# Expert layer in two table-driven loops with 64-row slots for the rests, first-layer weights fetched per tile

## The reference, cut to what matters

```python
h = jnp.mod(x_flat[:, :TOP_K].sum(axis=1).astype(jnp.int32), E)      # E = 8, TOP_K = 2
sel = jnp.stack([h, jnp.mod(h + 1, E)], axis=1)
w = jnp.any(sel == e, axis=1).astype(x.dtype) / TOP_K
y = jnp.maximum(x_flat @ W1e + b1e, 0.0) @ W2e + b2e                  # W1e 128x512, W2e 512x128
x = _layernorm(x + _L0_ffn_ref(x, ...))
```

| group | 0 | 1 | 2 | 3 | 4 | 5 | 6 | 7 |
|---|---|---|---|---|---|---|---|---|
| all 2048 tokens | 1052 | 324 | 132 | 35 | 10 | 29 | 131 | 335 |
| first 1536 tokens | 772 | 249 | 101 | 27 | 10 | 26 | 102 | 249 |

## Time and profile before

### The profile page before, as it was taken

The page is one execution under the profiler, slowest core; times in us unless marked ns, Lnnn a source line. Parts: engine busy times, 40 slices in busy tenths (PEclk is TensorE's granted clock), DMA queues, the critical chain, the costliest instruction groups (busy, mean ns, idle before and its releaser), DMA issues.

```text
span 236.5 us, 10737 instructions
## 1 busy us (share of the span) xinstructions
PE 212.2 (90%) x4009; PEld 176.2 (75%) x4009; DVE 147.3 (62%) x521; ACT 120.6 (51%) x360; POOL 117.8 (50%) x219
## 2 busy tenths in 40 slices
PE   6879999999998999998999988999999999999920
PEld 2445778767777667886776678989999999899920
DVE  6836448585877765888898616734655555555540
ACT  3546557765466646765656145754344434344400
POOL 6563034852544427762647601847646545455541
PEclk9999999999999999999999999999999999999995
DMA  4131120112232132130001365212121212121100
GB/s 100 58 94 47 49 96 3 45 52 91 91 78 66 47 103 72 43 96 15 28 25 36 117 201 151 96 38 76 40 62 44 56 43 57 27 48 36 35 22 7
DMA packets 18557, 14.73 MB, mean 62 GB/s; under 512 B 2647, under 2 KB 15547, under 8 KB 18513
## 3 DMA queue, kind: packets, MB, share of 16 engines
q1 hardware_dynamic: 17008, 11.83, 17.9%
q0 software_dynamic: 1216, 2.16, 2.8%
q10 hardware_dynamic: 288, 0.13, 0.3%
HBM read 11.43 MB, written 3.03 MB: 61 GB/s over the span
## 4 chain that ended last, share of the span: by engine, by line
PE 74%; DVE 6%; issue 5%; DMA 4%; POOL 3%; ACT 3%; SPq 1%; POOLq 0%; ACTq 0%; DVEq 0%
PE bS L1308 12%; PE bT L1251 7%; PE bV L1452 6%; PE bV L1459 5%; PE bS L1194 4%; PE bV L1266 4%; PE bS L1219 4%; PE bJ L1170 3%; PE bV L1323 3%; PE bT L1308 3%; PE bS L1233 2%; PE bL L1367 2%; PE bS L1201 2%; PE bV L1274 2%; DMA out<-yo,idx 2%
## 5 line engine op out<-in xcount | busy, mean ns | idle before, releaser
L680 ACT ACTIVATE ha<-bS,b1c 128x128 f32<-128x128 f32 x68 | 19.4, 368 | 38.0 <-PE bS L1308 38.0
L668 ACT COPY PTs<-bT 128x512 f32<-128x512 f32 (+3 forms) x48 | 25.9, 539 | 18.2 <-PE bT L1251 18.2
L567 POOL DMA_INDIRECT out<-yo,idx x18 | 19.4, 1076 | 17.5 <-POOL idx L563 9.6
L1251 PE MATMUL bT<-ident,Pr 128*128 128x128 f32 x168 | 27.2, 277 | 0.5 <-issue 0.4
L1308 PE MATMUL bS<-xsT,w_s 128*128 128x128 f32 x204 | 26.3, 279 | 1.1 <-issue 1.0
L1308 PEld LDWEIGHTS bS<-xsT,w_s 128*128 128x128 f32 x204 | 24.1, 192 | 2.2 <-issue 2.2
L498 POOL TENSOR_SCALAR rstd<-mv 128x1 f32<-128x1 f32 x16 | 3.8, 236 | 44.0 <-DVE mv L859 44.0
L1251 PEld LDWEIGHTS bT<-ident,Pr 128*128 128x128 f32 x168 | 19.5, 141 | 5.4 <-issue 4.1
L514 POOL DMA_INDIRECT groups<-x,pos x16 | 16.5, 1034 | 11.7 <-DVE pos L909 8.4
L655 ACT ACTIVATE Pr<-bS 128x512 f32<-128x512 f32 x32 | 20.1, 629 | 3.0 <-PE bS L1233 3.0
L814 DVE TENSOR_REDUCE mx<-bS 128x8 bf16<-128x512 f32 x32 | 21.4, 677 | 0.0
(11 more groups left out here) (237 smaller groups left out, 496.9 us busy)
## 6 DMA issues: line engine op xcount, KB each, us to landing
w_s<-in_L_ffn_W SPq DMA_DIRECT2D x16, 256.0 KB
w1f<-in_L_ffn_W SPq DMA_DIRECT2D x10, 256.0 KB, 3.0
xrow<-groups SPq DMA_DIRECT2D x22, 64.5 KB, 1.9
xs<-groups SPq DMA_DIRECT2D x18, 64.0 KB
x_tok<-in_L_attn_x SPq DMA_DIRECT2D x4, 256.0 KB, 3.7
groups<-padrows SPq DMA_DIRECT2D x1, 516.0 KB, 6.0
b2r<-in_L_ffn_b SPq DMA_DIRECT2D x1, 512.0 KB, 3.4
out<-yo,idx POOLq DMA_INDIRECT x18
```

What stands on the lines that cost most here:

```text
L567: nc.gpsimd.indirect_dma_start(rows_out, bass.IndirectOffsetOnAxis(ap=idx[:], axis=0), yo[:, FULL - 1, :], None, bounds_check=T * P - 1, o ...
L668: nc.scalar.copy(PTs[:, j, 0:m, :], bT[:, 0:m * P].rearrange("p (c q) -> p c q", c=m)).then_inc(turned_out, 1)
L680: nc.scalar.activation(dst[:, c, :], src[:, c * P:(c + 1) * P], ACT.Relu, bias=bias_of(c)).then_inc(relu, 1)
L1251: last = nc.tensor.transpose(bT[:, c * P:(c + 1) * P], Pr[:, t % 2, j, c * P:(c + 1) * P], ident[:])
```

## The change

Unrolled full tiles become four (FULL = 4). The remaining tiles are done in two loops: the first over the rest of the full tiles of the first 12 token tiles, the second over the full tiles that are complete with all tokens, and over rests of more than 64 rows. Each group's rest of up to 64 rows is a slot of 64 rows; two slots make a tile of 128 (`xt`), and eight passes, one per expert in the ORDER 1, 2, 3, 0, 4, 5, 6, 7, each multiply the two slots of the groups e - 1 and e. As the loops' expert is not known ahead, each loop tile's expert and row are loaded from a table, its first-layer weights are fetched by SyncE into `w1a` and `w1b`, and the second-layer weights and biases are addressed by a register. The tables are built on one partition. `full_biases` is gone. VectorE takes three of the four relus of hb in a loop tile (before two), ScalarE one. The order of TensorE around the last token tile changes.

```diff
-    BA = FC // 2
+    BA = 1
-    FULL = (EARLY * P - E * (P - 1) + P - 1) // P
+    FULL = (EARLY * P - E * (P - 1) + P - 1) // P - 1
+    TS = P // 2
+    TT = E // 2
+    ORDER = [1, 2, 3, 0, 4, 5, 6, 7]
...
+        w1a, w1b = sb("w1a", [P, F]), sb("w1b", [P, F])
...
+            def load_tile(k, row, e):
+                sp.wait_ge(kept, k * 16)
+                sp.wait_ge(xT_up, k)
+                sp.dma_start(xs[:], seg[bass.ds(row, P), 0:D]).then_inc(tile_in, 16)
+                sp.wait_ge(up_a, k)
+                sp.wait_ge(w1a_ok, k * 16)
+                sp.dma_start(w1a[:].unsqueeze(1), W1[bass.ds(e, 1)].rearrange("e p f -> p e f")).then_inc(w1a_ok, 16)
+                sp.wait_ge(up_b, k)
+                sp.wait_ge(w1b_ok, k * 16)
+                sp.dma_start(w1b[:].unsqueeze(1), W1[bass.ds((e + 1) % E, 1)].rearrange("e p f -> p e f")).then_inc(w1b_ok, 16)
+                sp.dma_start(xrow[:, bass.ds(k * XW, XW)], seg[bass.ds(row, P), :]).then_inc(kept, 16)
+
+            f1 = load_bound1(sp)
+            with sp.Fori(FULL, f1) as k:
+                load_tile(k, load_entry(sp, rows1, k, E * SEG - P), load_entry(sp, experts1, k, E - 1))
+            f2 = load_bound2(sp)
             sp.wait_ge(scattered_late, 16 * KT_)
+            with sp.Fori(f1, f2) as k:
+                load_tile(k, load_entry(sp, rows2, entry_of(k, f1), E * SEG - P),
+                          load_entry(sp, experts2, entry_of(k, f1), E - 1))
+            tail = load_table(sp, tail_table, range(E), tails_ok, E * SEG - TS)
+            sp.wait_ge(xT_up, f2)
             sp.dma_start(xs[:], seg[(E - 1) * SEG:(E - 1) * SEG + P, 0:D]).then_inc(tile_in, 16)
+            for g in range(E):
+                h = (g % 2) * TS
+                sp.dma_start(xt[h:h + TS, g // 2, :], seg[bass.ds(tail[g], TS), :]).then_inc(tail_in[g // 2], 16)
...
+            tail_deviation(0)
+            pool.wait_ge(out_in, f2 * 16)
+            tail_deviation(1)
+            tail_store(0)
+            tail_store(1)
+            tail_deviation(2)
+            tail_deviation(3)
+            tail_store(2)
+            tail_store(3)
...
+            for i, e in enumerate(ORDER):
+                h, src = (ha, bA) if i % 2 == 0 else (hb, bB)
+                act.wait_ge(slot_up, i + 1)
+                if i >= 2:
+                    act.wait_ge(slot_down, i - 1)
+                for c in range(FC):
+                    nc.scalar.activation(h[:, c, :], src[:, c * P:(c + 1) * P], ACT.Relu,
+                                         bias=bias_at(e)(c)).then_inc(slot_relu, 1)
...
-                if t == T + 2:
-                    keep_busy(6)
-                    columns(0)
-                    keep_busy(4)
-                    up_full(0, 0)
-                    pe.wait_ge(f_in, 32 * E)
-                    experts = load_table(pe, full_table[:, 0, :], [0, 1], full_ok, E - 1)
                 if t >= 3:
                     pe.wait_ge(gated, t - 2)
                     nc.tensor.transpose(aT, att[:], ident[:]).then_inc(attT_up, 1)
+                if t == T + 2:
+                    columns(0)
+                    pe.wait_ge(f_in, 32 * (E + 1))
+                    experts = load_table(pe, experts1, [0, 1], full_ok, E - 1)
...
+            def tile_of(e, k):
+                pe.wait_ge(w1a_ok, k * 16 + 16)
+                up(lambda c: bA, k, w1a, up_a)
+                pe.wait_ge(w1b_ok, k * 16 + 16)
+                up(lambda c: bB if c < BA else bC, k, w1b, up_b)
+                pe.wait_ge(loop_biased, k)
...
+            with pe.Fori(FULL, f1) as k:
+                tile_of(load_entry(pe, experts1, k, E - 1), k)
+            f2 = load_bound2(pe)
+            with pe.Fori(f1, f2) as k:
+                tile_of(load_entry(pe, experts2, entry_of(k, f1), E - 1), k)
...
+            def slot_pass_down(i):
+                e = ORDER[i]
+                h = ha if i % 2 == 0 else hb
+                groups = (0, E - 1) if e == 0 else (e - 1, e)
+                if i == 1:
+                    pe.wait_ge(loop_biased, f2)
+                for c in range(FC):
+                    pe.wait_ge(slot_relu, FC * i + c + 1)
+                    opens = [c == 0 and g not in opened for g in groups]
+                    if e % 2 and opens[0] == opens[1]:
+                        last = mm(slot_sum[e // 2][:, 0:D], h[:, c, :], w2_s[:, e, c, :], start=opens[0], stop=False,
+                                  skip_group_check=True)
+                        continue
+                    for q, g in enumerate(groups):
+                        r = (g % 2) * TS
+                        last = mm(slot_sum[g // 2][r:r + TS, 0:D], h[:, c, q * TS:(q + 1) * TS], w2_s[:, e, c, :],
+                                  start=opens[q], stop=False, skip_group_check=True)
...
+            tail_turn(0)
+            tail_turn(1)
+            for i in range(E):
+                slot_pass_up(i)
+                if i + 2 < TT:
+                    tail_turn(i + 2)
+                if i >= 1:
+                    slot_pass_down(i - 1)
+            slot_pass_down(E - 1)
```

More of the change, by code:

```diff
@@ L371, in _ @@
-            first = [FULL] + load_table(sp, tile_table[:, 0, :], [1], table_ok, T + E, FULL)
             sp.sem_inc(tile_in, 16 * FULL)
             sp.sem_inc(kept, 16 * FULL)
-            sp.wait_ge(scattered_late, 16 * KT_)
[L376 to L388, removed]
@@ L727, in _ @@
                     nc.scalar.copy(fsum[:, j, :], bY[:, 0:D]).then_inc(f_out, 1)
[L728 removed]
+            relus(hb, bB, HEAD, up_b, bias_of(experts[HEAD] + 1), BA)
             columns_copy(FULL)
[L730 to L740 removed]
+            relus(hb, bB, HEAD, up_b, bias_of(experts[HEAD] + 1), FC, BA)
@@ new lines, in _ @@
+            act.wait_ge(down, FULL)
+            nc.scalar.copy(fsum[:, HEAD, :], bY[:, 0:D]).then_inc(f_out, 1)
+            def tile_of(e, k):
+                act.wait_ge(up_a, k + 1)
+                act.wait_ge(full_ok, 1)
+                for c in range(FC):
+                    nc.scalar.activation(ha[:, c, :], bA[:, c * P:(c + 1) * P], ACT.Relu,
+                                         bias=bias_of(e)(c)).then_inc(relu, 1)
+                act.wait_ge(up_b, k + 1)
+                act.wait_ge(full_ok, 1)
+                for c in range(BA):
+                    nc.scalar.activation(hb[:, c, :], bB[:, c * P:(c + 1) * P], ACT.Relu,
+                                         bias=bias_of(e + 1)(c)).then_inc(relu, 1)
@@ L956, in count_tiles @@
[L956 to L970 removed]
+                return running([n, m, full[:, 2, :]])
@@ L1067, in _ @@
             dve.sem_inc(relu_b, FULL * (FC - BA))
[L1068 to L1086 removed]
+            dve.sem_inc(loop_biased, FULL)
@@ new lines, in tile_of @@
+            def tile_of(e, last):
+                k = last + 1
+                dve.wait_ge(up_b, k + 1)
+                dve.wait_ge(down, k)
+                for c in range(BA, FC):
+                    nc.vector.tensor_scalar(hb[:, c, :], bC[:, c * P:(c + 1) * P],
+                                            b1c[:, bass.ds(e * FC + FC + c, 1)], 0.0, ALU.add, ALU.max).then_inc(relu_b, 1)
+                column_copy(k + 1)
+                dve.wait_ge(out_in, last * 16)
+                dve.wait_ge(rs_ok, k)
+                finish(FULL - 1)
+                dve.wait_ge(kept, k * 16 + 16)
+                dve.wait_ge(down, k + 1)
+                summed_up(bL[:, 0:D], b2f[:, bass.ds(e * D, D)], loop_biased)
+                moments(k, FULL - 1, xrow[:, bass.ds(k * XW, D)], loop_biased)
@@ new lines, in tile_of @@
+            def tile_of(e, k):
+                pe.wait_ge(w1a_ok, k * 16 + 16)
[3 more added lines that the diff above has]
+                pe.wait_ge(loop_biased, k)
+                by_act = k * (FC + BA) + FULL * (FC - BA)
+                for c in range(FC):
+                    pe.wait_ge(relu, by_act + c + 1)
+                    mm(bL[:, 0:D], ha[:, c, :], w2f[:, bass.ds(e * F + c * P, P)], start=(c == 0), stop=False)
+                columns(k + 1)
+                for c in range(FC):
+                    if c < BA:
+                        pe.wait_ge(relu, by_act + FC + c + 1)
+                    else:
+                        pe.wait_ge(relu_b, k * (FC - BA) + c - BA + 1)
+                    last = mm(bL[:, 0:D], hb[:, c, :], w2f[:, bass.ds(e * F + F + c * P, P)], start=False,
+                              stop=(c == FC - 1))
+                last.then_inc(down, 1)
```

432 lines of the change are left out of this document (253 added, 179 removed).

## The result

The changed kernel took 255.98 us (median of 4 runs, 252.84 to 259.0), the kernel before 239.18 beside it (238.46 to 240.09). The ratio is 1.061, 95% interval 1.052 to 1.071. The forecast was 241.5 with a range to 247: the direction was right, the size was not, and the range did not hold the time. A second measurement of the unaltered changed kernel gave 254.76 against 238.68 (1.066, 1.063 to 1.070).

What follows compares the result with a forecast made beforehand. The prediction took TensorE to bound the old loops and SyncE's fetch chain the new ones. Start -4.5, loops and slots +7.1, end -0.1 gave +2.5 us of span, 241.5 us as median, range 235.5 to 247.

Steps and rivals of the forecast that it cites:

- The forecast's reading of before: Expert loops of the kernel before: bound by TensorE at 3.68 us per tile, with DMA engines nearly idle.
- Start: Last unrolled tiles before the loops: tile 3's transpose at 148.5 us, loop one starting at 155.0, 4.5 us earlier than before.
- To the first looped up: From tile 3's transpose to the first looped up: 6.5 us, with 0.3 waiting for hb and 0.6 for two loads.
- The period: Each loop tile: SyncE's serial chain of issues and xrow's landing sets 4.7 us, hiding TensorE's need of 4.13.
- First periods: First five loop periods: 23.2 us, with VectorE's late relu costing 0.7 us in one tile, absorbed by the chain.
- Passage to the slots: From the last looped up to the first slot's up: 7.5 us, with SyncE's eight register loads ahead of xs.
- Slots: Eight slot passes: 15.0 us, with a pair of 64-column halves costing one product plus 0.02 us.
- End: From TensorE's end to the end of the span: 10.1 us.
- Fetch hidden: Rival in the loops: TensorE stays the bound at 4.1 to 4.2 us per tile, total 235.5 us; chance 0.26.
- Halves serial: Rival in the slots: 64-column halves do not overlap, adding 4.0 us, total 245.5 us; chance 0.12.
- Fetch slower: Rival in the loops: slower landings make 5.3 us per tile, adding 6 us, total 247.5 us; chance 0.10.
- The warning sign named last: Sign that the forecast is wrong: TensorE's clock falls in the gaps, of which before's gaps of about 1 us gave no sign.

Runs made afterwards that it cites:

- the four kernels that ran next on the first chip: The changed kernel unaltered (1.066), with first-layer weights fetched once (1.039), with a fixed expert on TensorE (1.050), and with both of these changes (median 240.91 us).
- the order of the yo's: Changed kernel with VectorE taking the second and third unrolled tiles' last steps ahead of the fourth tile's sum: 263.21 us, ratio 1.072.
- two relus and the late load: Changed kernel with TensorE's entry load moved behind the ups and two relus each on ScalarE and VectorE: 257.21 us, ratio 1.048.
- The experiment: Changed kernel with SyncE issuing the last tile's xs before its eight register loads, each load just ahead of its tail transfer: 263.5 us, ratio 1.075.
- both edits: Changed kernel with first-layer weights fetched once and a fixed expert on TensorE (no entry load, constant addresses): median 240.91 us.

## Why the prediction was wrong

**The forecast's reading of before** stands: TensorE-bound loops, 3.68 us per tile, and nothing in the experiments speaks against it.

**Start: failed.** Tile 3's transpose, forecast at 148.5, came at 154.2. TensorE's code up to that place is the same in the four kernels that ran next on the first chip, and they gave 153.2, 150.6, 150.9 and 148.5: the forecast's figure is met where least went wrong. The rest is what it did not hold: in the profiled run a stretch of half clock (the 1.2 GHz level) near 14 to 21 us (attention's first output product is then at 36.4 us, 2.3 later than in before; in the four others of that chip it is at 33.6 to 34.1, so this was that execution's alone), the stop of 1.96 us at 104.3, and half clock again around 140 to 147 (0.66 over 137 to 147), behind two idle times:

```profile
139.61 0.33 PE L1520 MATMUL bL<-ident,att 128*128 128x128 f32 x1 [1.37 <-DVE att L978]
...
141.57 1.03 PE L1452 MATMUL bJ<-spare 128*128 128x256 bf16 x4 [1.31 <-issue]
...
142.82 3.62 PE L1479 MATMUL bS<-xsT,w1f 128*128 128x128 f32 x16
```

Sixteen records of ups take 3.62 us there, about 1.7 more than at full clock. The three add up to 6.0 us, for the 5.7 by which the transpose came late. The idle times do not decide the fall by themselves: the kernel with the weights fetched once has the same two (1.37 and 1.29) and a clock of 1.00 from 140 to 150 us. What decides it is open.

**To the first looped up: mis-sized**, 8.0 for 6.5. The wait for hb was 0.49 for 0.3; where 0.6 was taken for the two loads, 1.42 us is idle with issue alone ahead of the first looped ups.

**The period: the step that failed was "TensorE's own need is 3.68 + 0.45 for the entry's load = 4.13, hidden if the chain is 4.7".** SyncE's chain was sized rightly: 4.63 where it alone binds. TensorE's own need was not: with no fetch at all it is 4.96, over the chain that was to hide it. The 0.45 is one weight load's wait where a bound is loaded. With no fetch, the idle at the new loop's head is 0.77; products addressed by a register take 1.01 per eight records, which the forecast took at the 0.89 of before; and the ups behind the idle head take 2.05 with the last product's way out, where the row of before makes it 1.78. That is 0.32, 0.24 and 0.27 more, 4.96 where 4.13 was taken. With the fetch the pieces are the same and the idle at the head is 0.87 to 0.92, which makes 5.07. The fetch waits for the ups and the ups for the fetch, and I take the last 0.1 for that ring; three of the eight heads name w1a.

The price of an idle head could have been read more fully in the kernel before, in the timeline of TensorE:

```profile
202.79 1.60 PE L1308 MATMUL bS<-xsT,w_s 128*128 128x128 f32 x12 [0.32 <-issue]
...
207.13 1.60 PE L1308 MATMUL bS<-xsT,w_s 128*128 128x128 f32 x12 [0.40 <-issue]
...
210.91 1.50 PE L1308 MATMUL bS<-xsT,w_s 128*128 128x128 f32 x12
```

From one idle head to the next it is 4.34 us, 0.66 over 3.68. The forecast's own 66.8 us for 17 tiles say the same: 4.2 us over 17 times 3.68, in seven periods of 4.0 to 4.7. That would have given a need of about 4.3, still under 4.7; the rest, the longer idle in every tile and the register addresses, is in no row of before.

**First periods: failed.** The forecast had 0.7 us in one tile, to be absorbed by the chain; it became 6.1 us over five periods. The periods were 5.35, 6.72, 6.35, 5.74 and 5.11. Five at the steady 5.07 would already be 2.15 over the forecast's 23.2. The fourth has 0.67 more, and the idle behind it is 1.54 instead of 0.87: there the second loop begins and its bound is loaded too, which the forecast did not count. The third has 1.3 more, with its ups at half clock (3.5 us from the first to the downs, where 1.9 is usual). The second has 1.65 more, with 0.81 of waiting for VectorE's relu and 0.26 for ScalarE's. Why the relus are late there is open: in the unaltered kernel's second profile VectorE stands 3.1 us for a store to land, but the order of the yo's, which I took for the cause, is not it. Without the fetch the five take 26.7 and not 29.5, on the second chip with two relus and the late load 25.6.

**Passage to the slots: right**, 7.7 for 7.5, with SyncE's eight loads, xs late by 1.66 and xt by 0.90. The experiment adds that it can't be had back by order alone.

**Slots: mechanism right, size wrong.** Pairs of halves cost one record. The term that is missing is the change of width: at full clock four passes take 8.58 us (235.89 to 244.47), 2.14 each, where 15.0 over eight is 1.88. The Trainium skill (TensorEngine Tiling (Array Packing), Key Properties) says that a change of tiling mode drains TensorE; the rows agree, with 0.1 to 0.2 us at a change, and none where records of the same width follow. Over eight passes that is 2.1 of the 3.0 us; the first ups, 1.92 us at half clock, hold the rest.

**End: right**, 9.6 for 10.1.

**Rivals.** Fetch hidden: no, though taking it away gives 7.2 us of the whole. Halves serial: no. Fetch slower: its 247.5 was nearest, but by luck, since its mechanism is not there: w1a's issues to landing are

```profile
DMA to landing us min/median/max: 2.4/2.8/3.4
```

as forecast from w1f. The Trainium skill's formula (DMA: Bandwidth & Descriptors, Anatomy of one DMA) is given there for GpSimd's path, while these transfers are SyncE's; as an estimate it makes 2.6 of these 256 KB, which land in 2.8 (median), and 2.15 of the 64 KB of xs, which land in 1.8. But in the chain what counts is xrow behind the weights, 2.6 to 3.05. The warning sign named last, a clock that falls in the gaps, is part of what happened; that no stretch of before gives a sign was an argument from a kernel whose gaps were filled.

## What to carry to other kernels

Before a chain of one engine is called the bound, the other engine's loop has to be summed at its own new price: branch, register load, register arithmetic and addresses, with nothing hidden at the loop's head; here it was 4.96 against 4.63, and each hid the other from a single cut. Load a register where its first use lies behind queued work, not at the head: one moved load gave 0.44 us per tile. A change that adds small gaps to a tightly packed engine should be priced with falls of the clock too. In stretches that this change thinned out they cost 1.7, 1.3 and 0.9 of the 18.2 us, and not in every kernel with the same gaps. Another 2.3 us came with a fall in attention's code near 14 to 21 us, which only that execution of the first chip had, so it can't be put down to the change.

## What the runs showed of the hardware

A compare-and-branch in TensorE's queue measures 208 ns (median) and a register load 303 (297 to 328). At a loop's head, together with register arithmetic, they leave TensorE idle for 0.77 us without the fetch and 0.87 to 0.92 with it; the branch without the load leaves 0.05 (both edits) to 0.12 (the entry's load behind the ups). Switching between records of 128 and of 64 columns costs 0.1 to 0.2 us each time. The granted clock fell to half behind two idle times of 1.3 to 1.4 us with little work between them, but stayed at 1.00 behind the same two in three other kernels; it fell too near 174 us, behind 0.81 and 0.93 us idle, and near 229 us, behind 1.66 and 0.90. The loops, with 0.9 us idle in each 5.1, kept 0.99 from 177 to 217 us. Two chips differ by 3% on the kernel before, and in the profiles of the changed kernels the second one has two more idle stretches, of 1.9 and 2.7 to 2.8 us, in which ScalarE stands too and for which the profiles give no cause.
